# Second layer of a fused transformer kernel: score units of two planes alternate, and the value products go one key block at a time into four chunks

## What is computed

```python
x = L0_attn_encodings
xn = _layernorm(x, axis=-1)
x = x + _L0_attn_ref(xn, ...) + _L0_ffn_ref(xn, ...)
xn = _layernorm(x, axis=-1)
x = x + _L1_attn_ref(xn, L1_attn_Wq, L1_attn_Wkv, L1_attn_Wo) + _L1_ffn_ref(xn, L1_ffn_Wg, L1_ffn_Wu, L1_ffn_Wd)

# _L1_attn_ref: causal attention
sim = jnp.einsum('bhid,bhjd->bhij', q, k)
e = jnp.exp(jnp.where(causal_mask, mask_value, sim) - m)      # m: row maximum
out = jnp.einsum('bhij,bhjd->bhid', e, v) / (jnp.sum(e, axis=-1, keepdims=True) + eps)

# _L1_ffn_ref: for each of 8 experts
h = jax.nn.silu(x @ wg) * (x @ wu)      # 128 -> 512
acc = acc + h @ wd                      # 512 -> 128
```

## Time and profile before

| | us |
|---|---|
| median of 3 runs | 1380.21 |
| lowest and highest | 1377.72, 1387.30 |
| the profiled execution | 1377.35 |
| its span in the trace | 1375.6 |

### The profile page before, as it was taken

How to read it: one execution, slowest core, us unless ns; L and a number is a source line. 1 busy time by engine, 2 the same in 40 slices (tenths; PEclk the granted TensorE clock), 3 DMA queues, 4 the chain that set the end, 5 groups by cost and what they waited for, 6 DMA issues and landing times. The chain is left out here.

```text
span 1375.6 us, 23359 instructions
## 1 busy us (share of the span) xinstructions
PE 1290.5 (94%) x8254; PEld 767.0 (56%) x8262; DVE 1019.7 (74%) x2369; ACT 824.6 (60%) x1235; POOL 737.6 (54%) x859
## 2 busy tenths in 40 slices
PE   3899999999999988999999999999999999999996
PEld 1444455445454435665666666665666666666664
DVE  4576777777767656887887788788788788788764
ACT  1456676676776745666566566566566566566561
POOL 5153465645656435665655655655655654655551
PEclk8699999999999988999999999999999999999999
DMA  5222333424333221011111210110110111101002
GB/s 180 68 67 91 95 96 104 135 81 150 110 110 115 87 87 41 29 51 58 58 51 51 65 51 29 41 51 29 42 50 31 41 44 36 41 22 36 18 16 85
DMA packets 57282, 90.92 MB, mean 66 GB/s; under 512 B 12071, under 2 KB 22828, under 8 KB 57166
## 3 DMA queue, kind: packets, MB, share of 16 engines
q1 hardware_dynamic: 56014, 88.91, 20.5%
q10 hardware_dynamic: 1152, 0.52, 0.2%
HBM read 43.75 MB, written 44.53 MB: 64 GB/s over the span
## 5 line engine op out<-in xcount | busy, mean ns | idle before, releaser
L1242 POOL TENSOR_TENSOR a_h_lo<-a_h,a_h_hi 128x512 fp32r<-128x512 f32 x256 | 328.9, 1285 | 153.9 <-ACT a_h_hi L1314 153.1
L192 POOL TENSOR_SCALAR_AFFINE_SELECT E<-E 128x256 f32<-128x256 f32 (+1 forms) x384 | 195.0, 511 | 350.1 <-ACT E L1321 208.9
L695 DVE TENSOR_REDUCE mx<-bank_pair 128x2 f32<-128x1024 f32 (+3 forms) x264 | 209.2, 818 | 112.5 <-PE bank_pair L939 111.1
L1396 DVE SCALAR_TENSOR_TENSOR a_h<-a_h,bank_pair 128x512 f32<-128x512 f32 x256 | 175.2, 684 | 144.5 <-ACT a_h L1310 144.4
L1314 ACT ACTIVATE a_h_hi<-a_h 128x512 fp32r<-128x512 f32 x256 | 161.6, 631 | 128.4 <-DVE a_h L1402 125.6
L1321 ACT ACTIVATE E<-bank_pair 128x1024 f32<-128x1024 f32 (+1 forms) x192 | 169.6, 883 | 115.0 <-PE bank_pair L140 115.0
L168 DVE CUSTOM_DVE_ANT_0 bank_pair<-bank_pair,mask 128x512 f32<-128x512 f32 x496 | 230.6, 517 | 0.0
L133 PE MATMUL bank_pair<-st 24*128 24x512 f32 (+3 forms) x1024 | 200.5, 387 | 16.1 <-ACT E L781 3.8
L781 ACT ACTIVATE E<-bank_pair 128x1024 f32<-128x1024 f32 (+1 forms) x192 | 168.3, 878 | 68.1 <-PE bank_pair L140 66.4
L1402 DVE TENSOR_TENSOR a_h<-a_h,bank 128x512 f32<-128x512 f32 x256 | 176.1, 688 | 27.4 <-DVE a_h L1396 0.9
L1310 ACT ACTIVATE a_h<-bank_pair 128x512 f32<-128x512 f32 x256 | 151.1, 590 | 75.1 <-PE bank_pair L1537 73.7
(11 more groups left out here) (201 smaller groups left out, 2337.3 us busy)
## 6 DMA issues: line engine op xcount, KB each, us to landing
st<-stack_d SPq DMA_DIRECT2D x256, 96.0 KB
o_d<-O SPq DMA_DIRECT2D x64, 256.0 KB, 2.1
stack_d<-l_q_k_hi SPq DMA_DIRECT2D x56, 256.0 KB, 3.0
stack_d<-l_q_k_lo SPq DMA_DIRECT2D x28, 256.0 KB, 3.4
st<-ms SPq DMA_DIRECT2D x128, 8.0 KB
wst<-wg_in SPq DMA_DIRECT2D x8, 256.0 KB, 3.1
wst<-wu_in SPq DMA_DIRECT2D x8, 256.0 KB, 3.3
wst<-wd_in SPq DMA_DIRECT2D x8, 256.0 KB, 3.6
```

The source lines that it names most:

```text
L192: return nc.gpsimd.affine_select(out=part, in_=part, compare_op=ALU.is_ge, fill=0.0, base=0, pattern=pattern, channel_multiplier=-1)
L695: ins = nc.vector.tensor_reduce(out, pair[:, :, col:col + width(kb)], AX.X, ALU.max)
L1242: nc.gpsimd.tensor_tensor(h_lo[:, q % RH, :], h[:, q % RH, :], h_hi[:, q % RH, :].bitcast(F32), ALU.subtract).then_inc(h_lo_ready, 1)
L1396: nc.vector.scalar_tensor_tensor(hq, hq, 1.0, g_bank[:, :], ALU.add, ALU.mult).then_inc(silu_ready, 1)
```

## The change

The score order becomes `UNIT_ORDER = (0, 3, 1, 4, 2, 5)`, and keys, exponentials and masks now follow the same list, each one chunk behind the scores. So units of the two planes take turns: in every chunk the score unit and the key unit are of different planes. The value products of a quad no longer wait for the next round: block 0 goes into chunk 5 of the quad's own round, block 1 into chunk 6, block 3 into chunk 7 and block 2 into chunk 0 of the next round. Each waits for as many masked units as it needs (2, 4, 4 and 6 of 6), and the accumulation ends with block 2.

```diff
-SCORE_ORDER = (3, 4, 5, 0, 1, 2)
+UNIT_ORDER = (0, 3, 1, 4, 2, 5)
+VALUES_AT = {5: 0, 6: 1, 7: 3}
...
-def values_by_probs(nc, pv_bank, V, E, g, kb, slots):
+def values_by_probs(nc, pv_bank, V, E, g, kb, slots, last=NT - 1):
...
-                               E[:, (PLANES * g + j) % slots, at:at + w], start=kb == 0, stop=kb == NT - 1)
+                               E[:, (PLANES * g + j) % slots, at:at + w], start=kb == 0, stop=kb == last)
...
-            def causal(g, n):
-                pool.wait_ge(exp_done, UNITS_A_QUAD * g + n + 1)
+            def causal(g, m):
+                n = UNIT_ORDER[m]
+                pool.wait_ge(exp_done, UNITS_A_QUAD * g + m + 1)
...
-            def exp(g, n):
+            def exp(g, m):
+                n = UNIT_ORDER[m]
                 at_col, w, pair = EXP_AT[n % 3], EXP_WIDTH[n % 3], PLANES * g + n // 3
-                act.wait_ge(T_ready, UNITS_A_QUAD * g + n + 1)
+                act.wait_ge(T_ready, UNITS_A_QUAD * g + m + 1)
...
             def unit(g, i):
-                n = SCORE_ORDER[i]
+                n = UNIT_ORDER[i]
...
-                n = None if i is None else SCORE_ORDER[i]
+                n, key_unit = (None if k is None else UNIT_ORDER[k] for k in (i, m))
...
-                key_blocks = UNITS[m % 3] if here else []
+                key_blocks = UNITS[key_unit % 3] if here else []
...
             def PV(g, kb):
-                if kb == 0:
-                    pe.wait_ge(masked, UNITS_A_QUAD * (g + 1))
-                    if g > 0:
-                        pe.wait_ge(O_copied, g)
-                ins = values_by_probs(nc, pv_bank, V, E, g, kb, SLOTS_E)
-                if kb == NT - 1:
+                pe.wait_ge(masked, UNITS_A_QUAD * g + {0: 2, 1: 4, 3: 4, 2: 6}[kb])
+                if kb == 0 and g > 0:
+                    pe.wait_ge(O_copied, g)
+                ins = values_by_probs(nc, pv_bank, V, E, g, kb, SLOTS_E, 2)
+                if kb == 2:
                     ins.then_inc(pv_done, 1)
...
                     if back and n == 0:
-                        PV(g - 1, 0)
-                        PV(g - 1, 1)
-                    if back and n == 1:
                         PV(g - 1, 2)
-                        PV(g - 1, 3)
+                    if c in VALUES_AT:
+                        PV(g, VALUES_AT[c])
...
-            for kb in range(NT):
-                PV(QUADS - 1, kb)
+            PV(QUADS - 1, 2)
```

More of the change, by code:

```diff
@@ L1487, in scores_and_keys @@
                         if k < len(key_blocks):
-                            ins = keys_by_queries(nc, T_banks[:, r, :], stacks[g % STACKS], r, m // 3, key_blocks[k])
+                            ins = keys_by_queries(nc, T_banks[:, r, :], stacks[g % STACKS], r, key_unit // 3, key_blocks[k])
                             if r == HALVES - 1 and k == len(key_blocks) - 1:
```

## The result

| | before | after |
|---|---|---|
| median of 20 runs, us | 1381.67 | 1388.57 |
| profiled execution: span, us | 1375.6 | 1382.8 |
| of it, rounds 0 to 30 of the second layer | 804.9 | 811.5 |

The changed kernel takes 1.0047 times the time of before (95 % interval 1.0033 to 1.0061): about 6.5 us slower, where 2 us faster was forecast. The 6.6 us of the 31 full rounds carry it. So the question is which rounds are longer.

The account below looks back on a forecast made before the run. TensorE bounds the kernel, with waits that belong to VectorE. Work 24.02 plus waits 1.26 gives 25.28 us a round; four rounds save 0.24, eight times that 1.9: 1377.35 to about 1375.4, on the median's scale 1378, range 1361 to 1391.

Parts of the forecast that it names:

- The change on TensorE alone, 24.02 a round: TensorE's work in a plain round without waits: 24.02 us against 23.85 before, a loss of 0.17.
- rival 2: Chunks 5, 6, 7 and 0: turns to value products cost more, up to 0.6 us a round, 1391 to 1397; chance 0.10.
- Waits that go, waits that come: TensorE's waits: 0.85 us go in chunks 6, 7, 0 and 0.46 in 5; 1.26 come in chunks 2, 3, 4.
- Rival 1: Chunk 3's wait does not come: 1.13 us a round gained, 1342, or 1360 with half; chance 0.18, mostly the half form.
- The new plain round, 25.28: Plain round of the second layer: 24.02 us of work plus 1.26 of new waits.
- "0.21 less": Gain of a plain round: 25.28 us against 25.49 before.
- The four-round sum: Four rounds with weight split and late unit: 4 x 25.28 + 1.86 = 102.98 us against 103.22, 0.24 less.
- Other rounds, "0.6 in all": Extra work of weight split and late unit loses vanished waits of chunks 7 and 0: 0.6 us more per four rounds.
- The sign: Whole kernel slightly faster: 0.24 us less per four rounds, eight times that, 1.9 us.
- Rival 3: ScalarE late in chunk 4 delays chunk 5's gate 0.5 us in eight split rounds: 1382; chance 0.72 together with the forecast.

Follow-up runs that it names:

- Experiment 7: Changed kernel with value block 2 moved from chunk 0 to chunk 3, ahead of the scores, value bank copied a chunk later: 1372.07 us, 0.9907 of the kernel before.
- experiment 3: Changed kernel with VectorE's two small instructions on the softmax sums in chunk 7 instead of 6: 1383.17 us, 1.0013 of the kernel before.
- experiment 1: The changed kernel's unit order alone, value products back in chunks 0 and 1 of the next round: 1417.30 us, 1.0242 of the kernel before.

## Why the prediction was wrong, point by point

- *The change on TensorE alone, 24.02 a round*: right. Chunks 0, 5 and 6 came within 0.03 of it. Chunk 7, which I had put at 2.79, is 2.86: its maxima products take 0.33 to the value products (in the kernel before 0.24 to the down products), where I had estimated 0.15. The turns to value products cost 0.13 each, so rival 2 falls.
- *Waits that go, waits that come*: right; of the 1.26 that come, chunk 3's 0.99 measured 0.99, and chunks 2 and 4 are 2.90 and 2.87 for 2.87 and 2.88. Rival 1 falls. Experiment 7 shows that this wait was indeed idle time that could hold work, though nothing in the change filled it.
- *The new plain round, 25.28*: measured 25.27 to 25.33. The chunks agree one by one, so this was not luck.
- *"0.21 less" than 25.49 as a plain round's gain*: it compared with one kind of plain round. Before, the round behind a late unit was 25.2, since the unit also hid chunk 0's wait of 0.18; after, it is 25.3 like the others, so it loses 0.1 where I had it gain 0.21. The four-round sum was meant to repair this, but it carried the 0.21 over all four rounds.
- *Other rounds, "0.6 in all"*: this is the step that failed. I let the extra work of the weight split and the late unit grow from 1.26 to 1.86 in four rounds. The four rounds from 1125.50 to 1229.31 of the changed kernel last 103.81, against a forecast of 102.98: extras of 2.57 over four plain rounds of 25.31.

```profile
1125.50 0.39 PE L1537 MATMUL bank_pair<-xT_hi,a_w_hi 128*128 128x512 f32 x1
...
1229.31 0.39 PE L1537 MATMUL bank_pair<-xT_hi,w_hi 128*128 128x512 f32 x1
```

  Of the 0.71 missing, 0.51 is the small addition beside GpSimd (0.31 in chunk 7, 0.20 in the next chunk 0), which experiment 3 removes; the sum had no term for it. The other 0.2 is mostly the late unit. It adds 0.41 more to chunk 7 than before, where I had allowed 0.30. And both negations are held in its round, so that chunk 6 is 3.53 there and 3.36 elsewhere:

```profile
1196.87 1.25 DVE L181 TENSOR_SCALAR nm<-mx 128x16 fp32r<-128x16 f32 x1
1198.16 1.20 DVE L186 SCALAR_TENSOR_TENSOR nm<-mx,nm 128x16 fp32r<-128x16 f32 x1
```

  Against that, the 0.12 allowed for the weight split did not come: without the small addition its round is 0.75 above a plain one, before 0.78 above the 25.49. A further 0.12 is the plain rounds' own 0.03 four times.
- *The sign*: forecast 0.24 less in four rounds, measured 0.59 more (103.81 to 103.22). Rounds 12 to 30, nearly five such groups, carry 2.7 of the 6.6. The forecast took all 32 rounds for such groups, but rounds 1 to 10 have a late unit each. Rounds 1 to 11 carry 2.6, of which the small addition is 0.8 by experiment 3, and round 2 alone 1.2 (25.87 to 27.04). There VectorE's normalisation statistics, which no later round has, stand in front of chunk 2's silu. Chunks 2 and 3 now last 3.72 and 4.18, before 3.18 and 3.52, and chunk 3's gate waits 0.68, before 0.30. VectorE, then TensorE:

```profile
580.96 0.87 DVE L1432 BATCH_NORM_STATS2 stats<-xs 128x6 f32<-128x128 f32 x4
```

```profile
583.23 0.50 PE L1537 MATMUL bank_pair<-xT_hi,w_hi 128*128 128x512 f32 x1 [0.68 <-DVE a_h L1399]
```

  No experiment took this round's part out, so it stays read and not tested. Round 0's 1.2 is not told from noise.
- Rival 3 (ScalarE late in chunk 4, in the split rounds) is no new cost. In plain rounds nothing of it shows: chunk 4 is 2.87 and chunk 5 3.58. In the split round 16 chunk 4 is 3.15, so that chunk 5's gate is late by 0.28; but before, the same chunk was 3.30 in place of 2.73.

VectorE's small addition: the row shows 0.18 with GpSimd idle and 1.20 with a GpSimd instruction that had begun 0.14 earlier, and it ended 0.05 behind that one's end. The Trainium skill (SBUF — State Buffer, section SBUF: two separate sides) describes such a case: VectorE and GpSimd share one pair of ports, taken by an exclusive lock, which a VectorE instruction needs if it runs in a two-port mode or has two inputs in SBUF while GpSimd reads SBUF; whichever instruction starts first keeps it and the other blocks. The trace agrees with the order and with the end of the wait; in which mode the addition ran, no row shows. It would have been a rival had I asked on which side of GpSimd's 1.29 us instruction each SBUF-only instruction of VectorE would land. The trace of before had the sign: over the second layer the negation L185 on 16 columns had a mean of 1154 ns, its neighbour L180 of 215. The change did not remove that wait but moved it: after, the first negation is the long one.

Not every instruction on SBUF alone is held. The reciprocal behind the addition, on the same 64 columns, takes 0.55 in the changed kernel with GpSimd idle, and 0.55 before, where it began 0.01 ahead of GpSimd's instruction, which took its usual 1.29:

```profile
1065.98 0.55 DVE L1419 RECIPROCAL a_rden<-a_den 128x64 f32<-128x64 f32 x1
```

## What to carry to other kernels

A wait that a change removes may have been paying for something that happens only now and then: add up a whole period of the program, special rounds included, with every wait that is gone charged to the extra work that ran in it. Where an engine waits in program order, put independent work ahead of the waiting instruction, not behind it; here moving one value block, with the copy behind it a chunk later, turned a loss of 0.5 % into a gain of 0.9 %. And when an edit shifts VectorE against GpSimd, look at each VectorE instruction that touches SBUF alone and at what GpSimd runs at that moment.

## What was not expected of the hardware

- The two negations on 16 columns and the addition on 64, all on SBUF operands, last 0.17 to 0.22 us alone and 1.19 to 1.25 us when they start just behind a 1.29 us GpSimd instruction; they end 0.03 to 0.05 behind it. A reciprocal on the same 64 columns was not held. The silu and product instructions, which read PSUM for one operand, kept their 0.69 us beside the same GpSimd work.
- In experiment 1 a wait of TensorE of 1.69 us in an otherwise busy stretch was followed by a granted clock of 0.57 over the next 4 us, products 0.43 apart instead of 0.23. Waits of 1.54 to 1.72 stand in seven more rounds; two of these were followed by a lower clock (0.64 and 0.61), five by 1.00. The 0.99 us that chunk 3 waits in every round of the changed kernel left the clock at 1.00, as the row of the stretch 1100 to 1200 shows.
